# A norm's inverse root in the last stage: eleven Newton operations on VectorE, or one power on GpSimd a step later

## The reference

```python
def shift_tokens(t):
    a, s = jnp.split(t, 2, -1)
    s = jnp.pad(s, ((0, 0), (1, 0), (0, 0)))[:, :-1]
    return jnp.concatenate([a, s], -1)
def ffn_layer(x, g, bln, W1, b1, W2, b2):
    mu = x.mean(-1, keepdims=True)
    var = ((x - mu) ** 2).mean(-1, keepdims=True)
    xn = (x - mu) / jnp.sqrt(var + 1e-05) * g + bln
    hg = xn @ W1 + b1
    a, gate = jnp.split(hg, 2, -1)
    return a * jax.nn.gelu(gate, approximate=False) @ W2 + b2
for i in range(DEPTH):
    x = attn_layer(shift_tokens(x), Wqkv[i], q_scale[i], k_scale[i], Wo[i]) + x
    x = ffn_layer(shift_tokens(x), ln_g[i], ln_b[i], W1[i], b1[i], W2[i], b2[i]) + x
```

## Time and profile before

| | us |
|---|---|
| median of 3 runs (2869.9 to 2873.28) | 2872.33 |
| the profiled execution | 2870.53 |
| its span | 2868.4 |
| last stage's loop, from the first root to the end of the span | 1902.9 to 2868.4 |
| one job of it, in most cases | 41.67 |

### The profile page before, as it was taken

One profiled execution on the slowest core, in us unless ns is written; L12 is line 12 of the kernel. 1 busy time (PEld: TensorE's weight loads), 2 busy tenths in 40 slices (PEclk: granted clock), 3 DMA queues, 4 the chain that ended last, 5 costly groups with the idle time before them and its releaser, 6 DMA issues. The chain is left out here.

```text
span 2868.4 us, 57933 instructions
## 1 busy us (share of the span) xinstructions
PE 2533.2 (88%) x20585; PEld 1609.3 (56%) x20585; DVE 1777.3 (62%) x4074; ACT 1540.6 (54%) x4979; POOL 1363.8 (48%) x1981
## 2 busy tenths in 40 slices
PE   6999978988989979959289999689999999999996
PEld 3555545555645646646155555356666666666665
DVE  4556655545656755564645555677777777777773
ACT  1455534623746736623135555466667667666763
POOL 0344433401536623400004444587777777777772
PEclk8899997998989999989579999899999999999998
DMA  2000000000000010000010000200110101011000
GB/s 70 1 1 1 1 8 1 12 28 10 2 4 1 2 33 1 2 6 1 8 28 1 1 1 1 62 27 24 28 37 20 46 20 31 27 27 38 20 26 7
DMA packets 45711, 47.84 MB, mean 17 GB/s; under 512 B 11947, under 2 KB 31414, under 8 KB 45431
## 3 DMA queue, kind: packets, MB, share of 16 engines
q1 hardware_dynamic: 45430, 44.18, 5.6%
HBM read 31.05 MB, written 0.52 MB: 11 GB/s over the span
## 5 line engine op out<-in xcount | busy, mean ns | idle before, releaser
L1033 DVE TENSOR_REDUCE negmax<-scores 128x1 f32<-128x508 f32 (+4 forms) x512 | 212.6, 467 | 215.6 <-PE scores L918 184.4
L1013 POOL TENSOR_TENSOR l_xattn_probs<-l_xattn_probs,rowinv 128x512 f32<-128x512 f32 x128 | 130.3, 1039 | 421.1 <-DVE rowinv L1025 421.1
L2275 ACT ACTIVATE net_probs<-bank,net_negmax 128x96 f32<-128x96 f32 x768 | 251.7, 340 | 126.5 <-DVE net_negmax L2411 126.2
L1013 POOL TENSOR_TENSOR lora_probs<-lora_probs,rowinv 128x508 f32<-128x508 f32 (+1 forms) x256 | 149.5, 617 | 248.6 <-DVE rowinv L1025 248.6
L2329 POOL TENSOR_TENSOR net_rope<-net_rope,net_sin_parts 128x512 f32<-128x512 f32 x192 | 244.4, 1273 | 7.1 <-DVE net_sin_parts L2381 7.1
L2337 POOL TENSOR_TENSOR net_probs<-net_probs,net_inverse 128x384 f32<-128x384 f32 x192 | 158.7, 827 | 181.2 <-DVE net_inverse L2407 179.3
L2411 DVE TENSOR_REDUCE net_negmax<-bank 128x4 f32<-128x384 f32 x192 | 106.2, 553 | 196.0 <-PE bank L2109 195.3
L2350 POOL TENSOR_TENSOR net_rope<-net_rope,net_head_inv 128x512 f32<-128x512 f32 x192 | 201.2, 1048 | 7.5 <-POOL net_head_inv L1880 0.9
L124 DVE COPY turned<-flip 128x512 f32<-128x512 f32 (+3 forms) x280 | 163.2, 583 | 66.3 <-PE flip L945 52.3
L739 DVE TENSOR_REDUCE negmax<-scores 128x2 f32<-128x256 f32 (+2 forms) x192 | 157.8, 822 | 71.4 <-PE scores L647 42.0
L918 PE MATMUL scores<-kT,qM 64*128 64x512 f32 (+2 forms) x768 | 192.2, 577 | 6.0 <-ACT kT L122 2.5
(11 more groups left out here) (434 smaller groups left out, 6499.9 us busy)
## 6 DMA issues: line engine op xcount, KB each, us to landing
net_w_qkv<-in_L_ffn_Wqkv SPq DMA_DIRECT2D x12, 768.0 KB, 5.9
net_vals_between<-net_vals SPq DMA_DIRECT2D x48, 192.0 KB, 2.5
net_w_out<-in_L_ffn_Wo SPq DMA_DIRECT2D x6, 512.0 KB, 4.2
net_vals_between<-net_vals SPq DMA_DIRECT2D x48, 64.0 KB, 2.0
moe_w<-in_L_ffn_w13T SPq DMA_DIRECT2D x8, 256.0 KB, 2.7
net_w<-in_L_ffn_W SPq DMA_DIRECT2D x6, 341.0 KB
moe_w<-in_L_ffn_w2T SPq DMA_DIRECT2D x8, 128.0 KB, 2.3
ctx_tok<-in_ctx SPq DMA_DIRECT2D x1, 768.0 KB, 6.6
```

The costliest lines, as they stand in the source:

```text
L1013: last = nc.gpsimd.tensor_tensor(own, own, rowinv[:, u * tail + w:u * tail + w + 1].to_broadcast([P, k1 - k0]), ALU.mult)
L1033: last = nc.vector.tensor_reduce(negmax[:, u * tail + w:u * tail + w + 1], scores[:, 2 * qt + h, k0:k1], AX.X, ALU.max, negate=True)
L2275: last = nc.scalar.activation(prob_blocks(g)[:, w, :], score_blocks(g)[:, w // 2, w % 2, :], ACT.Exp, bias=maxima[:, g % 4, w:w + 1], accu ...
```

## The change

`root_of_variance` goes from DVE. In LATE, DVE only writes var + eps and -mean into the first two column groups of `ln_temp`, the third of which holds -0.5 from the beginning of the stage. One step later, at the end of its step, POOL raises the first to the third, and multiplies the second by the result. ACT waits for the same semaphore as before.

```diff
-                made = signal("window_made", 4)
+                made = signal("window_made", 5)
+                        nc.vector.memset(ln_temp[:, 2, :], -0.5).then_inc(made.sem, 1)
...
-            LN_OPS = 11
-            ln_rooted, normed = signal("net_ln_rooted", LN_OPS * JOBS), signal("net_normed", 2 * JOBS)
+            ln_ready, ln_rooted, normed = signal("net_ln_ready", 2 * JOBS), signal("net_ln_rooted", JOBS), signal("net_normed", 2 * JOBS)
...
+                        n = at_tick(s, LATE + 1, PER, JOBS)
+                        if n is not None:
+                            pool.wait_ge(ln_ready.sem, ln_ready.at(0, 2 * n + 2))
+
+                            until(pool, normed, 2 * n)
+                            nc.gpsimd.tensor_tensor(ln_inv[:, :], ln_temp[:, 0, :], ln_temp[:, 2, :], ALU.pow).then_inc(ln_rooted.sem, 1)
+                            pool.wait_ge(ln_rooted.sem, ln_rooted.at(0, n + 1))
+                            nc.gpsimd.tensor_tensor(ln_shift[:, :], ln_temp[:, 1, :], ln_inv[:, :], ALU.mult).then_inc(ln_shifted.sem, 1)
...
-                            root_of_variance(dve, n)
+                            until(dve, ln_rooted, n)
+                            nc.vector.tensor_scalar(ln_temp[:, 0, :], meanvar[:, 0:QT, 1], LN_EPS, None, ALU.add).then_inc(ln_ready.sem, 1)
+
+                            until(dve, ln_shifted, n)
+                            nc.vector.tensor_scalar(ln_temp[:, 1, :], meanvar[:, 0:QT, 0], -1.0, None, ALU.mult).then_inc(ln_ready.sem, 1)
```

More of the change, by code:

```diff
@@ L2382, in part @@
                                                 ALU.mult).then_inc(parted.sem, 1)
[L2384 to L2401, removed]
                     for s in TICKS:
```

## The result

| | before | after |
|---|---|---|
| median of 20 runs, us | 2866.95 (2855.3 to 2873.3) | 2876.22 (2866.1 to 2884.4) |
| profiled execution, us | 2870.53 | 2877.37 |
| its span, us | 2868.4 | 2875.6 |

The changed kernel is slower: its ratio to the kernel before is 1.0040, with a 95% interval of 1.0028 to 1.0053, so some 8 to 15 us. The forecast was 3.3 us less.

What follows compares the result with a forecast made beforehand. PE leads, with DVE's root on the path in every job; 22 (X - 0.51) - 1.9 + X - 1.72 = 23 X - 14.8, at X = 0.5 -3.3 us, so 2867.2 us from 2870.5; range 2862 to 2890.

Steps and rivals of the forecast that it cites:

- What bounds the kernel: Last stage: PE leads, and DVE's root is on the path in every job; removing it saves 2.06 us.
- The new wait: Step 7: ACT waits for POOL's multiply ahead of z, PE for z's transposes; L2171 moves by X - 0.51 us per job.
- X: Duration of the new power on POOL, shown by no row; taken as 0.5 us, break-even 0.64.
- 3.58 + X: Predicted new distance in us from POOL's row scaling to z's transposes on PE (L2171); the old one was 2.03.
- 23 X - 14.8: Predicted change of the whole time in us, all jobs and the drain summed; -3.3 at X = 0.5.
- From L2171 on the chain is again PE's own, so the whole shift of a job stays: Behind z's transposes on PE: each job's shift, X - 0.51 us, passes whole to the next root.
- (b): Rival: dear power, X over 0.89, at the end of POOL's step 6; at 1.2 +12.8, 2885.1 us; chance 0.32.
- (a): Rival: cheap power on POOL, X under 0.39; at 0.32 the time is 2864.9 us; chance 0.29.
- (c): Rival: the root does not hold POOL up, only the new wait stays; some +42 us, 2914; chance 0.02.
- The drain: Last two jobs of the stage: job 22 counted at -1.9 us, job 23 at X - 1.72 us.

Runs made afterwards that it cites:

- a4_bare: Changed kernel without POOL's block, root left out, DVE writing two stand-in values for ACT: 2804.5 us (before 2861.4), ratio 0.9789.
- c3_two_rounds: Kernel before with two rounds of Newton's iteration instead of three, the root less exact: 2836.2 us (before 2861.8), ratio 0.9907.
- b4_wait_alone: Kernel before, root kept on DVE, plus a power and a multiply on constants on POOL that ACT awaits: 2948.8 us (before 2862.6), ratio 1.0302.
- a2_floor: Changed kernel with the power replaced by a multiply of 128x2, root left out: 2846.7 us (before 2861.4), ratio 0.9946.

## Why the prediction was wrong

**What bounds the kernel: right.** a4_bare shows the root on the path whole, 2.10 us a job beside the 2.06 worked out, and c3_two_rounds that three of its operations are worth 0.59 us, three times their distance. One reading of the rows was wrong, and nothing rested on it: `ln_shift` was four microseconds old when ACT came to z (it is done at 2326.31, and z starts at 2330.51), not six.

**The new wait: right.** L2171 waits for ACT's z, and ACT for POOL, as foreseen. From the row scaling to L2171 it is 2374.45 - 2370.25 = 4.20 us, with the power's 0.72 in it: 3.48 + X where I had 3.58 + X. The fulfilled waits cost POOL nothing (2372.49 - 2371.26 = 1.23 from the adding to the power; I had 1.36). The order of the queues behind the waiting instructions was right, and ACT's copy was in time: it ends at 2376.16, and PE's scores start at 2376.47. Nothing else became late. With X = 0.72 the sum gives 0.21 us a job, and 0.15 were measured.

**X: mis-sized.** 0.72 us, not 0.5. The 0.3 for the function stood on no row. 23 X - 14.8 is then +1.8 us instead of -3.3. That by itself would still have been no change, within the forecast's own bounds for X (0.39 to 0.89). The runs show 0.52 us in its place, beside the 0.196 of the multiply of the same shape. By the factor of two of the Trainium skill (GPSIMD Engine Reference, Engine selection) X would have been an estimated 0.32, less than half of what the trace shows; the rule prices plain arithmetic, and for the multiply it is high as well (0.196 on POOL against 0.161 on DVE).

**The step that failed: "From L2171 on the chain is again PE's own, so the whole shift of a job stays".** The shift stays, but the chain behind L2171 does not keep its length. I replaced waits of 1.51 and 0.63 us on PE by waits of 0.33 and 2.00, and priced PE's work behind them as before. That work now runs at the lower clock in 11 of 21 jobs, which costs 1.56 us each time. The prediction had the slow jobs in view, as a disturbance of one job more or less, and miscounted them (six; the periods show 5 of 21). It did not ask what in the job they followed, although all five began their slow stretch at the same place, right behind PE's two longest waits. The kernel before, 2.5 us from the end of the second of them on, in a slow job and in the fast one of the earlier trace rows; the other four slow jobs have the 0.50 there too:

```profile
2161.65:2164.15 2.50, 2.50 (x12) 2.17 (x14) 2.16 (x4) 2.19 (x11) 2.50 (x3) 0.50 0.39 105
2331.19:2333.69 2.50, 2.50 (x24) 1.85 (x24) 2.30 (x5) 2.23 (x11) 2.50 (x3) 1.00 0.39 105
```

The measured 2876.2 us lies within the range of 2862 to 2890, but that is luck: no term of the sum has the clock in it, which made most of the difference.

**Rivals.** The time came out on the side of (b), but not by its mechanism: the power is not that dear, and with X = 0.72 the path alone cost 3 us in 21 jobs. Rival (a) falls with it too, and (c) is excluded by a4_bare.

**The drain.** In job 23 the first operation to ACT's z takes 1.32 us (2855.70 to 2857.02 in the changed kernel, against the 2.36 of the earlier trace rows); 0.64 + 0.72 = 1.36 were predicted. What job 22 gained can't be told apart: the period from job 22 to 23 lies between 23.3 and 31.0 us in these kernels, with the clock at either level in it.

## What to carry to other kernels

A wait that moves from one place to another at nearly the same length need not be neutral for TensorE: add up its idle time within the stretch where the new wait comes, and look at the granted clock of single jobs, not of the whole stage, before pricing the work behind it. When work goes to another engine, its place in that engine's queue is worth more than its duration; here the same change costs 0.4% with its two instructions in one place and gains 1.4% with them ten instructions earlier. Where such a gap can't be removed, work that nobody reads can fill it: here ten transposes left the period at full clock as it was (41.79 us beside 41.82) and no job was slow.

## What the runs showed of the hardware

**The more TensorE idles in the step, the more jobs fall to the lower clock.** In the thirteen kernels, PE's gaps in it sum to 0.31, 0.48, 1.21, 1.27, 1.32, 1.55 and 1.66 us with no slow job; to 1.78 with 3; 1.88 with 5; 2.14 with 5; 2.33 with 11; 3.09 with 19 of 21; and in b4_wait_alone 4.22 with 18, no more than at 3.09, but there the slow jobs are longer. The longest single wait does not order them: one of 1.66 us alone gave none, 1.47 with 0.31 ahead of it gave 3. Each number of slow jobs is from one execution, and so 3 and 5 are not told apart. What lets one job stay fast and the next, alike to 0.02 us, be slow was not found. It does not look like chance: counted from 0, the slow jobs are 3, 6, 9, 16 and 19 in the kernel before, 4, 10 and 16 in a2_floor, and every second one from 8 to 20 in the changed kernel. The Trainium skill (TensorE: Matmul & The Clock Gate, HAM oscillation) tells of a matmul kernel in which PE starts cold again behind every one of its waits for a DMA, longer ones than those here. The trace agrees that a wait can cost the clock of the work behind it (0.65 of full on average behind one of 2.0 us), but here only a part of the jobs is hit.

**A power on GpSimd** takes 0.69 to 0.73 us for 128x2 float32 values, an ordinary tensor-tensor operation of this size 0.20.
